# First node stage of a two-layer graph network: plain transposes, the split at PSUM, ReLU on ScalarE, the residual sum on GpSimd, the root for two tiles at once

## The chip, the cores and the metric

The kernel runs on one core of a Trainium2 chip. The metric is the device time of one execution in microseconds (us). The core has TensorE (PE in the profile; its weight loads are PEld), VectorE (DVE), ScalarE (ACT), GpSimd (POOL) and SyncE (SP), each with an instruction queue of its own that runs in order; they meet only at semaphores. In this kernel TensorE writes to PSUM, eight banks of 128 x 512 fp32, and everything else lies in SBUF or in the chip's DRAM.

## What is computed

10000 nodes with 512 features each, 10000 edges, two layers, each followed by a residual sum and a normalisation without learned scale:

```python
x = _layernorm(x + _L0_gnn_ref(x, edge_weight, W, b, edge_index))     # graph convolution
x = _layernorm(x + _L1_gnn_ref(x, src, dst, ...))                     # equivariant message layer

def _L0_gnn_ref(x, edge_weight, W, b, edge_index):
    ...
    norm = deg_inv_sqrt[src_all] * w_all * deg_inv_sqrt[dst_all]
    xp = x @ W
    out = segment_sum(xp[src_all] * norm[:, None], dst_all, N) + b    # self loops with weight 1
    return relu(out)

def _layernorm(x, eps=1e-05):
    return (x - mean(x)) / sqrt(var(x) + eps)
```

Only the part behind the segment sum of the first layer matters here. Since the sum and `@ W` commute, the kernel first sums the scaled neighbour rows into `sum0`, and then, node tile by node tile: z = sum0 + dis * x, y = relu(dis * (z @ W) + b) + x, x1 = layernorm(y).

## The kernel before

Nodes and edges are padded to 10240 = 80 tiles of 128 rows. There are five stages: constants and degrees, `edges0` (gather, TensorE combine, scatter-add into `sum0`), `nodes0` (the stage of the change), `edges1` (the second layer's messages, scatter-add into `sum1`) and `nodes1` (its node part). Each engine has its own program for each stage. `skewed` writes such a program as a software pipeline: in step s an engine does each of its parts for the tile s minus a lag, in the order in which the parts stand in its `nodes0` function. That order by hand is what sets when a part can run: an engine that waits holds up all that stands behind it.

`nodes0`, one tile a step. A lag is the number of steps behind the tile's load. All tiles are 128 x 512 fp32 unless said otherwise.

- SP: lag 0, loads `sl` (of `sum0`, ring of 4) and `xl` (of x, ring of 8), L366 and L368. Lag 8: stores x1 out of `res` to `x1_d` and to `sum1`, L372 and L373.
- DVE: lag 4, `pre`: L780, res = PSUM * dis + b. Lag 0, z: L786, sl = xl * dis + sl. Then again lag 4: L789, res = max(res, 0) + xl; L791 `bn_stats`; L793 `bn_aggr` into `mv`.
- ACT: lag 0, L567, z_hi = z rounded to fp32r. Lag 2: L556 and L561 copy the transposed high and low part from PSUM. Lag 5: L551 Ln and L559 Exp, the first guess of 1/sqrt(var + eps), 128 x 1. Lag 6: L571, the normalisation, res = res * scale + bias.
- POOL: lag 6, the five small operations of one Newton step on 128 x 1 (L458, L461, L463, L465, L467), then lag 0, z_lo = z - z_hi, L471.
- PE: lag 2, eight 128 x 128 fp32r multiplications with an identity (L984), four for z_hi and four for z_lo, into banks 0 to 3. Lag 3: twelve 128-row multiplications with 512 columns (L994): hi x Whi, hi x Wlo, lo x Whi for four chunks, into banks 4 to 7.

`Stage(sem, t, total)` counts the marks of a tile on one semaphore, `settle` waits for the engine's own last mark, `held` is a wait with a counting instruction behind it.

Of the kernel before, what the change touches and what calls it, by code (L numbers as in the profile page):

```python
# [85 lines left out]
def build(nc, x, src_cols, dst_cols, src_row, dst_row, weight, rbf, vec,  # L86
# [5 lines left out]
    with ExitStack() as ctx:  # L92
        def sb(name, shape, dt=F32):
            return ctx.enter_context(nc.sbuf_tensor(name, shape, dt))

        def sem(name):
            return ctx.enter_context(nc.semaphore(name))

        def ring(name, n, shape, dt=F32):
            return [sb(f"{name}{i}", shape, dt) for i in range(n)]  # L100
# [13 lines left out]
        ident_r = sb("ident_r", [P, P], F32R)  # L114
# [67 lines left out]
        sl, res, W0_s = ([b[:, q * D:(q + 1) * D] for b in node_mem] for q in range(3))  # L182
        xl = G
        z_hi, z_lo = (ring(name, 4, [P, D], F32R) for name in ("z_hi", "z_lo"))
        zT_hi, zT_lo = (ring(name, 2, [P, D], F32R) for name in ("zT_hi", "zT_lo"))
        stat = ring("stat", 4, [P, 6])
        mv = ring("mv", 4, [P, 2])
        tiny = ring("tiny", 4, [P, 8])
# [13 lines left out]
        msg_hi, msg_lo = z_hi, z_lo  # L202
# [63 lines left out]
        n_st = [sem(f"n_st{i}") for i in range(4)]  # L266
# [51 lines left out]
        K_RES, K_ROOT = 4, 5  # L318
# [7 lines left out]
        def _(sp_):  # L326
# [34 lines left out]
            def nodes0(s, u):  # L361
                a = u % 4
                if live(s, 0):
                    held(sp_, n_hi, s - 3)
                    held(sp_, n_lo, s - 3)
                    sp_.dma_start(sl[a], rows(sum0, s)).then_inc(n_sl[a], 16)  # L366
                    held(sp_, n_res, K_RES * (s - 7))
                    sp_.dma_start(xl[u], rows(x, s)).then_inc(n_xl[u], 16)  # L368
                if live(s, 8):
                    t = s - 8  # L370
# [4 lines left out]
            skewed(sp_, nodes0, 8, 8, unroll=8)  # L375
# [40 lines left out]
        def _(pool):  # L416
# [35 lines left out]
            def nodes0(s, u):  # L452
                if live(s, 6):

                    t, w, mean, var = s - 6, tiny[(u - 6) % 4], mv[(u - 6) % 4][:, 0:1], mv[(u - 6) % 4][:, 1:2]
# [7 lines left out]
                    st.mark(pool.tensor_scalar(w[:, 4:5], w[:, 3:4], -0.5, 1.5, ALU.mult, ALU.add))  # L463
                    st.settle(pool)
                    st.mark(pool.tensor_tensor(w[:, 5:6], w[:, 4:5], w[:, 2:3], ALU.mult))  # L465
                    held(pool, n_rstd, st.reached())
                    st.mark(pool.tensor_scalar(w[:, 6:7], mean, w[:, 5:6], -1.0, ALU.mult, ALU.mult))  # L467
# [39 lines left out]
        def _(act):  # L507
# [39 lines left out]
            def nodes0(s, u):  # L547
                if live(s, 5):
                    t, a = s - 5, (u - 5) % 4
                    act.wait_ge(n_res, K_RES * (t + 1))  # L550
                    act.activation(tiny[a][:, 1:2], mv[a][:, 1:2], ACT.Ln, bias=eps_c[:, :]).then_inc(n_rs, 1)  # L551
                if live(s, 2):
                    b = u % 2
                    act.wait_ge(n_tr, s - 1)
                    wait(act, n_mm, s - 3)
                    act.copy(zT_hi[b][:, :], bank[b][:, :]).then_inc(n_zT, 1)  # L556
                if live(s, 5):
                    act.wait_ge(n_rs, 2 * t + 1)
                    act.activation(tiny[a][:, 2:3], tiny[a][:, 1:2], ACT.Exp, scale=-0.5).then_inc(n_rs, 1)  # L559
                if live(s, 2):  # L560
                    act.copy(zT_lo[b][:, :], bank[2 + b][:, :]).then_inc(n_zT, 1)  # L561
                if live(s, 0):
                    a = u % 4
                    act.wait_ge(n_z, s + 1)
                    wait(act, n_tr, s - 3)
                    wait(act, n_lo, s - 3)
                    act.copy(z_hi[a][:, :], sl[a]).then_inc(n_hi, 1)  # L567
                if live(s, 6):
                    t, a = s - 6, (u - 6) % 4
                    act.wait_ge(n_rstd, K_ROOT * (t + 1))  # L570
                    act.activation(res[a], res[a], ACT.Identity, bias=tiny[a][:, 6:7], scale=tiny[a][:, 5:6]) \  # L571
                       .then_inc(n_x1, 1)

            skewed(act, nodes0, 6, 8, unroll=8)
# [87 lines left out]
        def _(dve):  # L662
# [20 lines left out]
            dve.tensor_scalar(ident_r[:, :], ident_i[:, :], 0.0, None, ALU.is_equal)  # L683
# [236 lines left out]
        def _(pe):  # L920
# [53 lines left out]
            def nodes0(s, u):  # L974

                if live(s, 2):
                    t, a, b = s - 2, (u - 2) % 4, u % 2
                    pe.wait_ge(n_hi, t + 1)
                    wait(pe, n_zT, 2 * (t - 1))
                    for part_, to in ((z_hi, bank[b]), (z_lo, bank[2 + b])):  # L980
                        if part_ is z_lo:
                            pe.wait_ge(n_lo, t + 1)
                        for c in range(4):
                            ins = pe.matmul(to[:, c * P:(c + 1) * P], part_[a][:, c * P:(c + 1) * P], ident_r[:, :],  # L984
                                            start=True, stop=True)
# [16 lines left out]
            pe.wait_ge(n_zT, 2 * T)  # L1002
            pe.wait_ge(n_res, K_RES * T)
# [117 lines left out]
```

## Time and profile before

| | |
|---|---|
| time, median of 3 runs | 1312.16 us (1312.09 to 1312.88) |
| the profiled execution, its own time | 1313.1 us |
| its span in the trace | 1311.3 us |
| first and last start of the `pre` operation (L780), 80 tiles | 360.5 and 655.7 us |
| PE, DVE, ACT, POOL busy in the whole span | 80%, 71%, 56%, 58% |
| TensorE clock, mean share of full speed | 0.896 |

The profile gives for each engine what ran when, and for each idle stretch what ended it. The shares of the whole span mix five stages with different limits. The stage of the change runs from about 349 to 662 us; it has to be read alone, and inside it one period of its loop. The start of an operation minus the start of the one before it on the same engine is what that one costs the engine; its duration is a little longer, since the end of one and the start of the next overlap.

### The profile page before, as it was taken

What the parts mean: (1) busy time and instruction counts of PE and PEld (TensorE: products, weight loads), DVE (VectorE), ACT (ScalarE), POOL (GpSimd) and SP (SyncE); (2) the same over time, 40 slices, a digit from 0 to 9 for tenths busy, and PEclk for the clock granted to TensorE, in tenths of its full rate; (3) what the DMA queues carried; (4) which work ended last, traced back from release to release, by engine and by line L of the source; (5) the groups of instructions that cost most, each with busy time, mean ns of one, the idle gap of its engine ahead of it and who ended that gap; (6) DMA issues with size and microseconds to landing.
All of it is one profiled execution on the core that took longest, in us unless ns stands there. A gap on an engine that the chain in (4) does not pass through costs nothing.

```text
span 1311.3 us, 27255 instructions
## 1 busy us (share of the span) xinstructions
PE 1049.4 (80%) x5208; PEld 783.2 (60%) x5208; DVE 928.9 (71%) x2936; ACT 735.9 (56%) x1852; POOL 756.5 (58%) x892
## 2 busy tenths in 40 slices
PE   7388778787599999999949999999999999514443
PEld 7343334343388888888738777776776777313332
DVE  8564354431188888888738888888888888529887
ACT  0111111111266667666648777777777777428887
POOL 0257777778367777777725666766766776410000
PEclk9998889898699999999969999999999999855555
DMA  9979999999757777777633556555555555369998
GB/s 366 412 193 218 222 217 212 211 222 181 205 187 258 265 258 263 262 260 264 207 114 80 104 107 103 107 103 104 104 104 107 102 105 107 51 148 328 347 354 288
DMA packets 164962, 257.37 MB, mean 196 GB/s; under 512 B 17514, under 2 KB 81470, under 8 KB 164926
## 3 DMA queue, kind: packets, MB, share of 16 engines
q0 software_dynamic: 35840, 83.91, 34.3%
q1 hardware_dynamic: 111902, 144.78, 33.9%
q10 hardware_dynamic: 17184, 28.32, 5.7%
q8 instruction: 10, 0.16, 0.1%
q14 instruction: 26, 0.21, 0.1%
HBM read 129.00 MB, written 127.93 MB: 196 GB/s over the span
## 4 chain that ended last, share of the span: by engine, by line
DMA 34%; issue 19%; POOL 10%; PE 3%; POOLq 2%; ACT 2%; DVE 2%; SPq 2%; ACTq 0%; DVEq 0%
DMA sum<-R_mem,sidx 30%; POOL tiny L458 3%; DMA node_mem<-sum 3%; POOL tiny L461 2%; POOL tiny L465 1%; PE bank L994 1%; POOL tiny L463 1%; DMA sum<-R_mem,sidx_all 1%; POOL z_lo L471 1%; POOLq L313 1%; POOL sum L444 1%; POOLq L314 1%; SPq L408 1%; ACT node_mem L649 1%; POOL tiny L467 0%
## 5 line engine op out<-in xcount | busy, mean ns | idle before, releaser
L963 PE MATMUL bank<-G_mem,edge_mem 128*128 128x512 f32 x400 | 196.4, 650 | 49.1 <-DMA G_mem<-x,src_i 49.1
L500 POOL DMA_INDIRECT sum<-R_mem,sidx x80 | 127.1, 1589 | 138.7 <-DMA sum<-R_mem,sidx 95.6
L534 ACT COPY R_mem<-bank 128x512 f32<-128x512 f32 x80 | 46.9, 586 | 227.5 <-PE bank L963 201.8
L963 PEld LDWEIGHTS bank<-G_mem,edge_mem 128*128 128x128 f32 x400 | 81.8, 209 | 151.2 <-issue 134.5
L485 POOL TENSOR_TENSOR z_lo<-edge_mem,z_hi 128x512 fp32r<-128x512 f32 x80 | 145.3, 1816 | 18.8 <-ACT z_hi L608 18.8
L444 POOL DMA_INDIRECT sum<-R_mem,sidx_all x80 | 127.5, 1594 | 45.1 <-issue 26.1
L994 PE MATMUL bank<-W0h,zT_hi 128*128 128x512 f32 x320 | 133.3, 417 | 0.8 <-ACT zT_lo L561 0.8
L994 PE MATMUL bank<-W0l,zT_hi 128*128 128x512 f32 x320 | 126.0, 394 | 0.0
L994 PE MATMUL bank<-W0h,zT_lo 128*128 128x512 f32 x320 | 126.0, 394 | 0.0
L761 DVE TENSOR_SCALAR edge_mem<-trow,dst_f,coef 128x512 f32<-128x512 int32 (+1 forms) x80 | 31.8, 459 | 130.2 <-PE bank L963 120.5
L571 ACT ACTIVATE node_mem<-node_mem,tiny 128x512 f32<-128x512 f32 x80 | 65.4, 817 | 92.1 <-POOL tiny L467 92.1
L471 POOL TENSOR_TENSOR z_lo<-node_mem,z_hi 128x512 fp32r<-128x512 f32 x80 | 103.7, 1297 | 21.1 <-ACT z_hi L567 21.1
L618 ACT ACTIVATE G_mem<-G_mem,ew 128x512 f32<-128x512 f32 x80 | 57.8, 723 | 95.2 <-DMA G_mem<-x_d,gidx 95.1
L786 DVE SCALAR_TENSOR_TENSOR node_mem<-G_mem,dis,node_mem 128x512 f32<-128x512 f32 x80 | 82.0, 1025 | 40.8 <-DMA G_mem<-x 40.8
L811 DVE TENSOR_SCALAR proj<-G_mem,Y 128x128 f32<-128x128 f32 x80 | 85.6, 1070 | 29.6 <-ACT G_mem L618 27.6
L1067 PE MATMUL bank<-ident,node_mem 128*128 128x128 f32 x80 | 27.4, 446 | 91.3 <-DVE node_mem L892 91.3
L492 POOL DMA_INDIRECT G_mem<-x_d,gidx x80 | 85.8, 1072 | 23.6 <-issue 17.0
L1031 PE MATMUL bank<-h,Wf_s 128*128 128x128 f32 x640 | 92.1, 288 | 3.2 <-DVE edge_mem L853 2.9
L430 POOL DMA_INDIRECT G_mem<-x,src_i x80 | 79.5, 994 | 24.2 <-issue 21.2
L1025 PE MATMUL bank<-edge_mem,Winv 128*128 128x512 f32 x160 | 90.8, 650 | 0.0
L780 DVE SCALAR_TENSOR_TENSOR node_mem<-bank,dis,b_s 128x512 f32<-128x512 f32 x80 | 60.0, 750 | 38.3 <-DMA sum<-node_mem 29.6
L1031 PEld LDWEIGHTS bank<-h,Wf_s 128*128 128x128 f32 x640 | 82.3, 198 | 5.7 <-issue 4.8
(161 smaller groups left out, 2896.2 us busy)
## 6 DMA issues: line engine op xcount, KB each, us to landing
sum<-zeros ACTq DMA_DIRECT2D x42, 512.0 KB, 11.4
node_mem<-sum SPq DMA_DIRECT2D x80, 256.0 KB, 2.7
G_mem<-x SPq DMA_DIRECT2D x80, 256.0 KB, 2.8
x_d<-node_mem SPq DMA_DIRECT2D x80, 256.0 KB, 2.1
sum<-node_mem SPq DMA_DIRECT2D x80, 192.0 KB, 2.0
out<-G_mem SPq DMA_DIRECT2D x20, 512.0 KB, 4.3
out<-R_mem SPq DMA_DIRECT2D x20, 512.0 KB, 4.4
G_mem<-sum SPq DMA_DIRECT2D x20, 384.0 KB, 5.1
```

The lines of the kernel that those rows point to most:

```text
L430: pool.indirect_dma_start(G[k][:, :], None, x, bass.IndirectOffsetOnAxis(ap=src_i[:, t:t + 1], axis=0)) \
L444: pool.indirect_dma_start(sum0, bass.IndirectOffsetOnAxis(ap=sidx[:, t:t + 1], axis=0), R[t % 8][:, :], None, compute_op=ALU.add).then_inc ...
L471: pool.tensor_tensor(z_lo[u][:, :], sl[u], z_hi[u][:, :].bitcast(F32), ALU.subtract).then_inc(n_lo, 1)
L485: pool.tensor_tensor(msg_lo[a][:, :], msg[a % 2][:, P:640], msg_hi[a][:, :].bitcast(F32), ALU.subtract) \
L492: pool.indirect_dma_start(G3[a][:, :], None, x1_d, bass.IndirectOffsetOnAxis(ap=gidx3[a][:, :], axis=0)) \
L500: pool.indirect_dma_start(sum1, bass.IndirectOffsetOnAxis(ap=sidx3[a][:, :], axis=0), R3[a][:, :], None, compute_op=ALU.add).then_inc(f_sc ...
L786: dve.scalar_tensor_tensor(sl[c], xl[u], dis[:, bass.ds(s, 1)], sl[c], ALU.mult, ALU.add).then_inc(n_z, 1)
L811: sj.mark(dve.tensor_scalar(proj[a][:, :], gv[:, :, 0], Y[:, bass.ds(t, 1), 0], None, ALU.mult))
L963: ins = pe.matmul(bank[j][:, :], M[c][q][:, j * P:(j + 1) * P], G[4 * c + q][:, :], start=(q == 3), stop=(q == j))
L994: ins = pe.matmul(bank[4 + a][:, :], zt[b][:, c * P:(c + 1) * P], w[:, c, :], start=(c == 0 and k == 0), stop=(c == 3 and k == 2))
L1025: pe.matmul(bank[2][:, :], Winv[:, :], rawT[b][:, 0:512], start=True, stop=True)
L1031: ins = pe.matmul(bank[4][:, q * P:(q + 1) * P], Wf2_s[:, base:base + 255:2], h[b][:, :], start=True, stop=True)
```

## The change

In `nodes0` of the first layer only:

- z is no longer split before the transposes. PE transposes z itself as fp32, four `transpose` instructions with `ident` instead of eight multiplications with `ident_r`; lag 1. The bank ring for it is 0 to 3, one bank for a tile.
- ACT copies the bank to zT_hi (rounding); DVE computes zT_lo = bank - zT_hi. z_hi, z_lo, ACT's L567 and L561 and POOL's L471 are gone; zT_hi and zT_lo are rings of 4.
- DVE writes `pre` (L780's operation); ACT does ReLU on `res` in place; POOL adds xl in place; DVE then takes `bn_stats` and `bn_aggr`. DVE's L789 is gone.
- Ln, Exp and the Newton step run once for a pair of tiles, on 128 x 2; seven small operations on POOL with six waits in between or before, no pointer scalars.
- `res` has 8 buffers, the stores have 8 semaphores, stores come at lag 9, the normalisation at lag 8.

The order within a step is new on each engine:

```diff
@@ gpsimd, nodes0
-                if live(s, 6):
-                    st = Stage(n_rstd, t, K_ROOT)
-                    held(pool, n_res, K_RES * (t + 1))
-                    st.mark(pool.tensor_scalar(w[:, 0:1], var, EPS, None, ALU.add))
-                    held(pool, n_rstd, st.reached())
-                    held(pool, n_rs, 2 * (t + 1))
-                    st.mark(pool.tensor_scalar(w[:, 3:4], w[:, 2:3], w[:, 2:3], w[:, 0:1], ALU.mult, ALU.mult))
...
-                if live(s, 0):
-                    pool.wait_ge(n_hi, s + 1)
-                    wait(pool, n_tr, s - 3)
-                    pool.tensor_tensor(z_lo[u][:, :], sl[u], z_hi[u][:, :].bitcast(F32), ALU.subtract).then_inc(n_lo, 1)
+                if live(s, 6) and u % 2:
+                    t, a = s - 7, (u - 7) // 2 % 4
+                    held(pool, n_mv, t + 2)
+                    st.mark(pool.tensor_scalar(w[:, 0, :], var, EPS, None, ALU.add))
+                    st.mark(pool.tensor_scalar(w[:, 7, :], mean, -1.0, None, ALU.mult))
+                    held(pool, n_rs, 2 * (g + 1))
+                    st.mark(pool.tensor_tensor(w[:, 3, :], w[:, 2, :], w[:, 2, :], ALU.mult))
+                    st.settle(pool)
+                    st.mark(pool.tensor_tensor(w[:, 4, :], w[:, 3, :], w[:, 0, :], ALU.mult))
+                    held(pool, n_rstd, st.reached())
+                    st.mark(pool.tensor_scalar(w[:, 3, :], w[:, 4, :], -0.5, 1.5, ALU.mult, ALU.add))
+                    st.settle(pool)
+                    st.mark(pool.tensor_tensor(w[:, 5, :], w[:, 3, :], w[:, 2, :], ALU.mult))
+                    st.settle(pool)
+                    st.mark(pool.tensor_tensor(w[:, 6, :], w[:, 7, :], w[:, 5, :], ALU.mult))
+                if live(s, 4):
+                    pool.wait_ge(n_rel, t + 1)
+                    pool.tensor_tensor(res[a], res[a], xl[a], ALU.add).then_inc(n_sum, 1)
@@ scalar, nodes0 (Ln and Exp of the pair stand ahead of and behind the zT_hi copy)
+                    act.wait_ge(n_tr, t2 + 1)
+                    wait(act, n_mm, t2 - 3)
+                    act.copy(zT_hi[b][:, :], bank[b][:, :]).then_inc(n_hi, 1)
...
+                if live(s, 4):
+                    act.wait_ge(n_pre, t4 + 1)
+                    act.activation(res[c], res[c], ACT.Relu).then_inc(n_rel, 1)
+                if live(s, 8):
+                    act.wait_ge(n_rstd, K_ROOT * (g8 + 1))
+                    act.activation(res[c], res[c], ACT.Identity, ...).then_inc(n_x1, 1)
@@ vector, nodes0
                 if live(s, 0):
                     dve.scalar_tensor_tensor(sl[c], xl[u], dis[:, bass.ds(s, 1)], sl[c], ALU.mult, ALU.add).then_inc(n_z, 1)
+                if live(s, 5):
+                    dve.wait_ge(n_sum, t + 1)
+                    dve.bn_stats(stat[c][:, :], res[a]).then_inc(n_bn, 1)
+                if live(s, 2):
+                    dve.wait_ge(n_hi, t + 1)
+                    wait(dve, n_mm, t - 3)
+                    dve.tensor_tensor(zT_lo[b][:, :], bank[b][:, :], zT_hi[b][:, :].bitcast(F32), ALU.subtract).then_inc(n_lo, 1)
+                if live(s, 5):
+                    if k == 0:
+                        held(dve, n_x1, t - 6)
+                    held(dve, n_bn, t + 1)
+                    dve.bn_aggr(mv[b][:, k, :], stat[a % 4][:, :]).then_inc(n_mv, 1)
                 if live(s, 4):
-                    st.settle(dve)
-                    st.mark(dve.scalar_tensor_tensor(res[a], res[a], 0.0, xl[(u - 4) % 8], ALU.max, ALU.add))
...
+                    dve.wait_ge(n_mm, t + 1)
+                    wait(dve, n_st[a], 32 * turn(t, a, 8))
+                    dve.scalar_tensor_tensor(res[a], bank[4 + c][:, :], dis[:, bass.ds(t, 1)], b0_s[:, :],
+                                             ALU.mult, ALU.add).then_inc(n_pre, 1)
@@ tensor, nodes0 (lag 1: four transposes; lag 3: the eight products with zT_hi, a wait for n_lo, the four with zT_lo)
+                    for c in range(4):
+                        ins = pe.transpose(bank[a][:, c * P:(c + 1) * P], sl[a][:, c * P:(c + 1) * P], ident[:, :])
```

## Rows read from the trace of the kernel before

**Rows 1.** Windows: us, busy us (instructions) by engine, TensorE clock, DMA share, GB/s.
```profile
500.00:620.00 120.00, 120.00 (x641) 102.89 (x640) 102.19 (x161) 81.94 (x193) 89.80 (x193) 1.00 0.77 262
```

**Rows 2.** Chain of work that ended last, 499 to 508 us, shares by line.
```profile
by line: issue 58.2%; POOL tiny L458 11.9%; POOL tiny L461 8.7%; POOL z_lo L471 4.9%; POOL tiny L465 4.5%; POOL tiny L463 4.3%; POOLq L313 3.4%; POOL tiny L467 2.1%; POOLq L314 2.1%; POOLq L74 0.7%; POOLq L469 0.7%
```

**Rows 3.** Timeline of POOL: start, duration (us), engine, line, operation; idle before.
```profile
500.61 0.53 POOL L458 TENSOR_SCALAR tiny<-mv 128x1 f32<-128x1 f32 x1
...
502.08 0.19 POOL L463 TENSOR_SCALAR tiny<-tiny 128x1 f32<-128x1 f32 x1 [0.20 <-POOL tiny L461]
...
502.76 0.26 POOL L467 TENSOR_SCALAR tiny<-mv,tiny 128x1 f32<-128x1 f32 x1 [0.21 <-POOL tiny L465]
502.98 1.31 POOL L471 TENSOR_TENSOR z_lo<-node_mem,z_hi 128x512 fp32r<-128x512 f32 x1
504.37 0.53 POOL L458 TENSOR_SCALAR tiny<-mv 128x1 f32<-128x1 f32 x1
```

**Rows 4.** Timeline of PE, same stage: first transpose, first product, next tile's transpose.
```profile
504.35 0.56 PE L984 MATMUL bank<-ident_r,z_hi 128*128 128x128 f32 x4
...
505.23 0.49 PE L994 MATMUL bank<-W0h,zT_hi 128*128 128x512 f32 x1
...
508.07 0.56 PE L984 MATMUL bank<-ident_r,z_hi 128*128 128x128 f32 x4
```

**Rows 5.** Timeline of PE in `edges1`: two plain fp32 transposes, back to back.
```profile
904.82 0.27 PE L1017 MATMUL bank<-ident,proj 128*128 128x128 f32 x1
...
904.93 0.27 PE L1018 MATMUL bank<-ident,G_mem 128*128 128x128 f32 x1
```

**Rows 6.** Timeline of DVE in `nodes0`, 388 to 392 us.
```profile
388.32 0.68 DVE L789 SCALAR_TENSOR_TENSOR node_mem<-node_mem,G_mem 128x512 f32<-128x512 f32 x1
389.04 0.69 DVE L791 BATCH_NORM_STATS2 stat<-node_mem 128x6 f32<-128x512 f32 x1
389.88 0.18 DVE L793 BATCH_NORM_AGGREGATE mv<-stat 128x2 f32<-128x6 f32 x1 [0.15 <-DVE stat L791]
390.01 0.75 DVE L780 SCALAR_TENSOR_TENSOR node_mem<-bank,dis,b_s 128x512 f32<-128x512 f32 x1
390.68 1.40 DVE L786 SCALAR_TENSOR_TENSOR node_mem<-G_mem,dis,node_mem 128x512 f32<-128x512 f32 x1
```

**Rows 7.** Lines by form (count, busy us, mean ns, idle): two DVE operations with a PSUM operand.
```profile
L900 DVE TENSOR_TENSOR R_mem<-bank,node_mem 128x256 f32<-128x256 f32 x20 | 8.4, 419 | 0.2
L853 DVE SCALAR_TENSOR_TENSOR edge_mem<-bank,bf_c,edge_mem 128x384 f32<-128x384 f32 x70 | 42.6, 608 | 0.0
```

**Rows 8.** Timeline of the stage's start: the first tile from DVE to ACT to POOL.
```profile
348.85 0.75 DVE L786 SCALAR_TENSOR_TENSOR node_mem<-G_mem,dis,node_mem 128x512 f32<-128x512 f32 x1 [38.92 <-DMA G_mem<-x]
349.64 0.62 ACT L567 CAST z_hi<-node_mem 128x512 fp32r<-128x512 f32 x1 [7.87 <-DVE node_mem L786]
...
350.34 1.26 POOL L471 TENSOR_TENSOR z_lo<-node_mem,z_hi 128x512 fp32r<-128x512 f32 x1 [11.11 <-ACT z_hi L567]
```

**Rows 9.** Instructions of line 571: count, duration min/median/max (ns), first and last start.
```profile
L571 ACT ACTIVATE node_mem<-node_mem,tiny x80: 813/817/820, 371.1 to 661.1; 128x512 f32<-128x512 f32 x80
```

**Rows 10.** Timeline of POOL: the subtraction that runs beside L786 of rows 6.
```profile
390.23 1.31 POOL L471 TENSOR_TENSOR z_lo<-node_mem,z_hi 128x512 fp32r<-128x512 f32 x1
```

**Rows 11.** Instructions of line 780: count, duration min/median/max (ns), first and last start.
```profile
L780 DVE SCALAR_TENSOR_TENSOR node_mem<-bank,dis,b_s x80: 749/750/753, 360.5 to 655.7; 128x512 f32<-128x512 f32 x80
```

**Rows 12.** Timeline of PE at the stage's start, low clock: two products in a row.
```profile
356.94 0.63 PE L994 MATMUL bank<-W0l,zT_hi 128*128 128x512 f32 x1
...
357.36 0.63 PE L994 MATMUL bank<-W0h,zT_lo 128*128 128x512 f32 x1
```

**Rows 13.** Windows of `edges0` and `edges1`, columns as in rows 1.
```profile
190.00:200.00 10.00, 6.19 (x8) 2.64 (x9) 2.98 (x16) 1.17 (x2) 7.88 (x7) 0.51 1.03 220
720.00:740.00 20.00, 18.28 (x113) 13.97 (x113) 16.69 (x60) 15.24 (x41) 12.74 (x11) 1.00 0.57 108
```

More of the change, by code:

```diff
@@ L181, in build @@
         node_mem = ring("node_mem", 4, [P, 4 * D])
-        sl, res, W0_s = ([b[:, q * D:(q + 1) * D] for b in node_mem] for q in range(3))
+        sl, W0_s = ([b[:, q * D:(q + 1) * D] for b in node_mem] for q in (0, 2))
+        res = [b[:, q * D:(q + 1) * D] for q in (1, 2) for b in node_mem]
         xl = G
-        z_hi, z_lo = (ring(name, 4, [P, D], F32R) for name in ("z_hi", "z_lo"))
-        zT_hi, zT_lo = (ring(name, 2, [P, D], F32R) for name in ("zT_hi", "zT_lo"))
+        zT_hi, zT_lo = (ring(name, 4, [P, D], F32R) for name in ("zT_hi", "zT_lo"))
         stat = ring("stat", 4, [P, 6])
-        mv = ring("mv", 4, [P, 2])
-        tiny = ring("tiny", 4, [P, 8])
+        mv = ring("mv", 4, [P, 2, 2])
+        tiny = ring("tiny", 4, [P, 8, 2])
         trow3 = ring("trow3", 4, [P, P], I32)
@@ L201, in build @@
         M3 = ring("M3", 4, [P, P], F32R)
-        msg_hi, msg_lo = z_hi, z_lo
+        msg_hi, msg_lo = zT_hi, zT_lo
         junk3 = ring("junk3", 4, [P, P])
@@ L265, in build @@
         n_x1 = sem("n_x1")
-        n_st = [sem(f"n_st{i}") for i in range(4)]
+        n_st = [sem(f"n_st{i}") for i in range(8)]
         f_trow = [sem(f"f_trow{i}") for i in range(4)]
@@ L373, in nodes0 @@
                     sp_.dma_start(sum1[bass.ds(t * P, P), C:D], res[a][:, C:D]).then_inc(n_st[a], 16)
[L375 removed]
+            skewed(sp_, nodes0, 9, 16, unroll=8)
             def edges1(s, u):
@@ L478, in _ @@
+                    st.settle(pool)
+                    st.mark(pool.tensor_tensor(w[:, 6, :], w[:, 7, :], w[:, 5, :], ALU.mult))
+                if live(s, 4):
+                    t, a = s - 4, (u - 4) % 8
+                    pool.wait_ge(n_rel, t + 1)
+                    pool.tensor_tensor(res[a], res[a], xl[a], ALU.add).then_inc(n_sum, 1)
+            skewed(pool, nodes0, 8, 16, unroll=8)
+            for u in range(8):
+                held(pool, n_st[u], 32 * (T // 8))
             held(pool, s_zero1, 16 * (T4 + 4))
@@ L547, in nodes0 @@
             def nodes0(s, u):
[L548 to L551, printed above, removed]
-                if live(s, 2):
[L553 to L571, printed above, removed]
+                tail = live(s, 6) and u % 2
+                if tail:
+                    t, a = s - 7, (u - 7) // 2 % 4
+                    g = t // 2 if isinstance(t, int) else (t - (u - 7) % 8) // 2 + a
+                    act.wait_ge(n_mv, t + 2)
+                    act.activation(tiny[a][:, 1, :], mv[a][:, :, 1], ACT.Ln, bias=eps_c[:, :]).then_inc(n_rs, 1)
@@ new lines, in nodes0 @@
+                if live(s, 2):
+                    t2, b = s - 2, (u - 2) % 4
+                    act.wait_ge(n_tr, t2 + 1)
+                    wait(act, n_mm, t2 - 3)
+                    act.copy(zT_hi[b][:, :], bank[b][:, :]).then_inc(n_hi, 1)
+                if tail:
+                    act.wait_ge(n_rs, 2 * g + 1)
+                    act.activation(tiny[a][:, 2, :], tiny[a][:, 1, :], ACT.Exp, scale=-0.5).then_inc(n_rs, 1)
+                if live(s, 4):
+                    t4, c = s - 4, (u - 4) % 8
+                    act.wait_ge(n_pre, t4 + 1)
+                    act.activation(res[c], res[c], ACT.Relu).then_inc(n_rel, 1)
@@ L572, in nodes0 @@
+                if live(s, 8):
+                    t8, c = s - 8, u % 8
+                    k, b = c % 2, c // 2
+                    g8 = t8 // 2 if isinstance(t8, int) else (t8 - c) // 2 + b
+                    act.wait_ge(n_rstd, K_ROOT * (g8 + 1))
+                    act.activation(res[c], res[c], ACT.Identity, bias=tiny[b][:, 6, k:k + 1], scale=tiny[b][:, 5, k:k + 1]) \
                        .then_inc(n_x1, 1)
-            skewed(act, nodes0, 6, 8, unroll=8)
+            skewed(act, nodes0, 8, 16, unroll=8)
@@ L974, in nodes0 @@
             def nodes0(s, u):
[L976 to L985, printed above, removed]
+                if live(s, 1):
+                    t, a = s - 1, (u - 1) % 4
+                    pe.wait_ge(n_z, t + 1)
+                    wait(pe, n_lo, t - 3)
+                    for c in range(4):
+                        ins = pe.transpose(bank[a][:, c * P:(c + 1) * P], sl[a][:, c * P:(c + 1) * P], ident[:, :])
@@ L986, in nodes0 @@
                     ins.then_inc(n_tr, 1)
                 if live(s, 3):
-                    t, a, b = s - 3, (u - 3) % 4, (u - 3) % 2
-                    pe.wait_ge(n_zT, 2 * (t + 1))
-                    wait(pe, n_res, K_RES * (t - 3))
+                    t, a = s - 3, (u - 3) % 4
+                    pe.wait_ge(n_hi, t + 1)
+                    wait(pe, n_pre, t - 3)
                     for c in range(4):
-                        for k, (zt, w) in enumerate(((zT_hi, W0h), (zT_hi, W0l), (zT_lo, W0h))):
-                            ins = pe.matmul(bank[4 + a][:, :], zt[b][:, c * P:(c + 1) * P], w[:, c, :],
-                                            start=(c == 0 and k == 0), stop=(c == 3 and k == 2))
+                        for w in (W0h, W0l):
+                            pe.matmul(bank[4 + a][:, :], zT_hi[a][:, c * P:(c + 1) * P], w[:, c, :],
+                                      start=(c == 0 and w is W0h), stop=False)
@@ L996, in nodes0 @@
+                    pe.wait_ge(n_lo, t + 1)
+                    for c in range(4):
+                        ins = pe.matmul(bank[4 + a][:, :], zT_lo[a][:, c * P:(c + 1) * P], W0h[:, c, :],
+                                        start=False, stop=(c == 3))
                     ins.then_inc(n_mm, 1)
             skewed(pe, nodes0, 3, 8)
-            pe.wait_ge(n_zT, 2 * T)
-            pe.wait_ge(n_res, K_RES * T)
+            pe.wait_ge(n_lo, T)
+            pe.wait_ge(n_pre, T)
             pe.wait_ge(s_wTc, 3)
```

51 lines of the change are left out of this document (20 added, 31 removed).

## The prediction, made from the kernel before

> **What bounds the kernel now.** I read the windows by stage first, since only one stage changes. Inside `nodes0` TensorE is busy all the time at its full clock, DVE 85% of it, POOL 75%, DMA 77% [rows 1]. A full TensorE looks like the bound, but its ends are modelled, so I looked at the chain of work next. It runs through POOL alone: its five small operations and z_lo; the large share called issue is the time in which POOL works off z_lo, and it always ends where L458 starts [rows 2]. The timeline of POOL gives the period: L458 starts at 500.61 and again at 504.37, 3.76 us. Of this 2.37 us go to the small operations (to 502.98) and 1.39 to z_lo [rows 3]. PE needs 0.88 us for eight multiplications with the identity and 2.84 us for twelve products, 3.72 together, so it stands only just behind POOL [rows 4]. Over the stage: `pre` starts first at 360.5 and last at 655.7, (655.7 - 360.5)/79 = 3.737 us a tile [rows 11]. That is the period I have to replace.
>
> **The parts, and what each engine would need.** All by start-to-start distances, which are a duration less some 0.08 us (`pre` lasts 0.75 and the next starts 0.67 later [rows 6]).
>
> PE: four plain transposes start 0.11 us apart in the later stage [rows 5], so about 0.44 plus 0.1 of run-in in place of 0.88; with 2.84 for the products, 3.4 us. The products' order doesn't matter for their sum.
>
> POOL: z_lo goes (-1.39), the addition comes. It is the same form, two SBUF operands, 128 x 512, and z_lo took 1.26 alone and 1.31 beside DVE [rows 8, 10]: 1.30, or 1.39 start to start. The small operations: five became seven, but for two tiles. A first one of 0.53 at most, a second of 0.26 (like L467), a wait of 0.20, then five at (502.76 - 502.08)/2 = 0.34 each [rows 3] with their waits: 2.7 us a pair. Twice the width (128 x 2) I cost at nothing: one element a row takes 0.19 us (L463), 512 take 1.31, so an element more is about 2 ns [rows 3]. POOL then needs 1.39 + 1.35 = 2.7 us a tile instead of 3.76.
>
> ACT: loses the z_hi cast (0.62) and the zT_lo copy, gains ReLU, SBUF to SBUF, 128 x 512. The nearest rows are the z_hi cast, 0.62 [rows 8], and the normalisation with two pointer operands, 0.82 [rows 9]. ReLU has no such operands: 0.62, bounds 0.57 to 0.82. ACT was busy 82 of 120 us, 2.6 of 3.75 a tile, so it has room [rows 1].
>
> DVE: loses L789 (0.68), gains zT_lo with one PSUM operand. 256 columns of this operation take 0.419 us; 384 columns of a three-operand one take 0.608 and 512 take 0.75, so 1.1 ns a column [rows 6, 7]. 0.419 + 256 x 1.07 ns = 0.69 us, 0.60 start to start; bounds 0.53 and 0.67 (from 0.75). DVE's sum is z 0.66, bn_stats 0.61, zT_lo 0.60, bn_aggr 0.12, pre 0.67 = 2.7 us, up to 3.3 where z waits for POOL.
>
> DMA moves the same bytes: 0.77 of 3.75 us, so 2.9 us a tile at least. Its waits (loads ahead by some steps, the store's 8 buffers for 4) get looser; the wait of `pre` for the store goes, and it bound nothing, as the chain is POOL's.
>
> So by work alone the tile would take 3.4 us (PE).
>
> **What the new order makes of it.** The parts of one tile t now pass from engine to engine and back. DVE writes pre(t) as the last thing of step t+4. ACT's ReLU(t) waits for it, POOL's addition(t) waits for ReLU(t), and DVE's bn_stats(t) waits for the addition. But bn_stats(t) stands in step t+5, with only z between it and pre(t). DVE runs in order, so zT_lo(t+3), bn_aggr(t) and pre(t+1) queue behind that wait. This closes a loop, one tile a turn, that no engine's speed but only the sum of latencies sets. Before, ReLU and residual followed pre on DVE itself (L789) and the statistics too, so no such loop was there. From pre's start:
>
> pre 0.75 + hand-over to ACT 0.04 (349.60 to 349.64) + ReLU 0.62 + hand-over to POOL 0.08 (350.26 to 350.34) [rows 8] + addition 1.30 + hand-over to DVE 0.05 (between those two) + bn_stats 0.61 (0.69 less 0.08) + zT_lo 0.60 + bn_aggr 0.13 (389.88 to 390.01 [rows 6]) = 4.18 us.
>
> z (0.66 from pre's start, lasting 0.75 alone) is over 1.41 us after pre's start, before the addition begins at 1.49: hidden. The other members are ready in time: ACT's zT_hi copy comes after ReLU and the normalisation, some 1.4 us behind ReLU's end, while DVE needs it 1.4 + 0.6 behind it. PE has 3.4 us of work in 4.2.
>
> Where the paired root falls: in odd steps POOL does it between two additions. The loop leaves it 4.18 - 1.30 = 2.88 us, and it needs 0.09 + 2.7. It just fits, with 0.1 us to spare. What could push it out is DVE's z: L786 lasted 1.40 instead of 0.75 us while z_lo ran beside it, and ended 0.54 behind z_lo's end [rows 6, 8, 10]; so one of the two was held off by the other. In the new order z starts about 2.05 us behind the end of an addition, where the last small operations run; one of them held off for up to 0.7 us would end the root near 3.1 and delay every second addition by 0.2 to 0.3. I take half of that, 0.07 a tile on the mean of both parities. The Trainium skill (SBUF — State Buffer, section "SBUF: two separate sides") says that DVE with two SBUF inputs and GpSimd share a port pair as an exclusive lock, the loser blocking for a whole instruction. The 1.40 us agree with that. By this rule the larger figure would hold: a small operation caught behind z costs all the rest of z.
>
> Period: 4.18 + 0.07 = 4.25 us.
>
> Head and tail: pre(0) starts about when it did (360.5; one fewer dependence on POOL, perhaps a us earlier). After pre(79) now come 0.79 + 0.70 + 1.35 + 0.70 + 0.15 + 0.18 + the root's 2.2 + two normalisations 1.6 = 7.7 us; before, from 655.7 to the end of the last L571 at 661.9, 6.2 [rows 9, 11]. A us either way: 0.
>
> **Sum.** 79 x (4.25 - 3.737) = +40.5 us against the profiled execution's 1313.1, whose own span is 1311.3 and which lies 0.9 above the median of the runs. On the median: 1312.2 + 40.5 = **1352.7 us**, 3.1% slower. Other stages: nothing changes in them but the names of two buffer rings and four more waits, under a us.
>
> **Rivals.**
>
> 1. No loop binds. If the wait of bn_stats were met early (a queue deeper than I think, or if I misread which tile the addition serves), PE sets 3.4 us: 79 x (3.4 - 3.737) = -27, 1286 us. For it: every engine's sum falls. Against: the indices, t+4 for pre and addition, t+5 for bn_stats, with z alone between. Chance 0.05, and 0.02 that loop and savings happen to balance within 0.2%.
>
> 2. The root sticks out on odd steps. If z catches it, or ReLU is as slow as the normalisation (0.82), or zT_lo takes 0.67, the turn is 4.18 + 0.20 + 0.07 + 0.06 (addition 1.36) + up to 0.25 = 4.76 us: +81, 1393 us. It decides as soon as the root takes over 2.8 us. Chance 0.13, together with the milder forms of it from 1370 upwards.
>
> 3. TensorE's clock falls. It will idle about 0.85 us of each 4.25, where it didn't idle before. At the low level (1.2 GHz) products start 0.42 us apart instead of 0.23 [rows 12], 12 x 0.42 + 1 = 6.1 us a tile, over the loop. For it: in `edges0` the clock was 0.51 in a stretch in which PE was busy 62% and its loads 26% [rows 13]. Against: in `edges1` loads were busy 70% and the clock held at 1.00 [rows 13], and the new stage has 16 loads of some 0.19 us in 4.25, 71%. With half of the stage at the low level: 79 x 0.5 x (6.1 - 4.25) = +73 more, about 1425 us. Chance 0.05. The Trainium skill (TensorE: Matmul & The Clock Gate, section "Part 4: PE-mode transpose") says that transposes of this mode don't count as activity for the clock; before they were ordinary multiplications. No row here isolates that; `edges1` has five such transposes a tile and held its clock.
>
> The forecast itself has 0.75. Its own range: all hand-overs at nothing and ReLU and zT_lo at their lower ends give 4.0 us, +21, 1333; ReLU at 0.75 with a late root gives 4.47, +58, 1370. Rivals 1 and 3 are left out of the range, most of rival 2 is taken in: **1332 to 1390**. A measurement of this kernel can tell 0.2%, 2.6 us, from no change. Faster by more than that 0.05, within it 0.02, slower 0.93.
>
> **What would show it.** In the profile after: the starts of `pre` 4.2 to 4.3 us apart; DVE idle before bn_stats, released by POOL's addition, some 1.4 us in each step (2.84 less 1.41); the chain going DVE, ACT, POOL, DVE; POOL idle before the addition in even steps and hardly in odd ones; PE with idle of 0.8 us a tile at a clock of 1.00. Wrong if DVE's bn_stats doesn't wait (rival 1), if POOL has no idle and odd steps are much longer than even ones (rival 2), or if the clock in the stage is below 0.9 (rival 3).

## The result

The changed kernel takes 1374.72 us, median of four runs (1372.81 to 1376.3), the kernel before beside it 1312.52 us: a ratio of 1.0473 (95% interval 1.0452 to 1.0494), 4.7% slower. Forecast were 1352.7 us and a range of 1332 to 1390. The sign and the range held; of the +62 us the forecast had 40.5, and the loop that it named turned out to be the second limit, not the first.

All of it lies in the stage of the change. The first and the last `pre` answer to [rows 11]; the operation has moved to line 803 (columns: count, duration min/median/max in ns, first and last start in us):

```profile
L803 DVE SCALAR_TENSOR_TENSOR node_mem<-bank,dis,b_s x80: 710/718/752, 358.5 to 717.3; 128x512 f32<-128x512 f32 x80
```

(717.3 - 358.5)/79 = 4.54 us a tile instead of 3.737; 79 x 0.805 = 63.6 us, and the span grew by 63.2 (1311.3 to 1374.5). The window that answers to [rows 1]:

```profile
500.00:520.00 20.00, 15.33 (x72) 11.24 (x70) 10.79 (x20) 9.62 (x19) 9.75 (x19) 1.00 0.62 216
```

No engine is at its limit: PE is busy 77%, DVE 54%, ACT 48%, POOL 49%, DMA 62%, and the clock is still full. So something waits in a circle. Who waited for whom in the stage (380 to 660 us; total us, times, longest), the last line from the same view of SyncE's DMA queue:

```profile
ACT node_mem L570 <- DVE node_mem L803: 161.4, 61, 3.2
POOL node_mem L476 <- ACT node_mem L570: 130.2, 61, 3.7
DVE node_mem L782 <- DMA G_mem<-x: 113.1, 61, 2.6
...
SPq L316 <- ACT node_mem L576: 136.1, 61, 3.0
```

The forecast had DVE waiting before bn_stats. It waits before z (L782) instead, for a load, once in each of 61 steps. In [rows 6] z followed pre without a gap. And SyncE's queue waits for ACT's normalisation (L576). The timelines of the four queues over two turns:

```profile
499.26 0.72 DVE L803 SCALAR_TENSOR_TENSOR node_mem<-bank,dis,b_s 128x512 f32<-128x512 f32 x1
...
500.01 0.63 ACT L570 ACTIVATE node_mem<-node_mem 128x512 f32<-128x512 f32 x1 [2.52 <-DVE node_mem L803]
500.55 0.80 ACT L576 ACTIVATE node_mem<-node_mem,tiny 128x512 f32<-128x512 f32 x1
...
501.59 0.35 SPq L373 DMA_DIRECT2D x_d<-node_mem  x1
502.14 0.36 SPq L374 DMA_DIRECT2D sum<-node_mem  x1
502.76 0.35 SPq L367 DMA_DIRECT2D node_mem<-sum  x1
503.30 0.35 SPq L369 DMA_DIRECT2D G_mem<-x  x1
...
505.29 1.30 POOL L476 TENSOR_TENSOR node_mem<-node_mem,G_mem 128x512 f32<-128x512 f32 x1 [3.27 <-ACT node_mem L570]
...
506.45 0.75 DVE L782 SCALAR_TENSOR_TENSOR node_mem<-G_mem,dis,node_mem 128x512 f32<-128x512 f32 x1 [1.90 <-DMA G_mem<-x]
507.12 0.69 DVE L786 BATCH_NORM_STATS2 stat<-node_mem 128x6 f32<-128x512 f32 x1
507.72 0.68 DVE L791 TENSOR_TENSOR zT_lo<-bank,zT_hi 128x512 fp32r<-128x512 f32 x1
508.31 0.17 DVE L798 BATCH_NORM_AGGREGATE mv<-stat 128x2 f32<-128x6 f32 x1
508.40 0.72 DVE L803 SCALAR_TENSOR_TENSOR node_mem<-bank,dis,b_s 128x512 f32<-128x512 f32 x1
```

By the starts: pre to ReLU 0.75, ReLU 0.54, normalisation to the first store 1.04, two stores and the load of `sl` to the load of `xl` 1.71, load to z 3.15, z 0.67, bn_stats 0.60, zT_lo 0.59, bn_aggr 0.09, and the second pre: 499.26 to 508.40, 9.14 us. Between them lies one more pre (503.83), so the circle has two turns: 4.57 us a tile. The order of the queues closes it: SyncE issues the load of step s behind the store that waits for the normalisation of ACT's step s-2, and that normalisation stands behind ReLU, which waits for pre of the same step. The addition ends at 506.59, 0.53 us before bn_stats starts, so z's wait for the load is the one that ends last here; what either is worth, the runs below show. (The chain-of-work view does not help: between 500 and 514 us it stays on POOL, 73.6% "issue" and 19.7% addition.)

### The profile page after: what moved, and what is told of

Read it like the earlier page. It is cut to its first block, busy times and chain, and to the rows that moved or that the text cites. A ratio compares the mean times of both kernels' runs of the same rounds, so it can differ in the third digit from the quotient of the medians.

```text
span 1374.5 us, 25149 instructions
## 1 busy us (share of the span) xinstructions
PE 1026.2 (75%) x4888; PEld 735.1 (53%) x4888; DVE 894.5 (65%) x2935; ACT 685.7 (50%) x1692; POOL 701.7 (51%) x772
## 4 chain that ended last, share of the span: by engine, by line
DMA 33%; issue 25%; POOL 7%; PE 4%; DVE 3%; ACT 2%; SPq 1%; POOLq 1%; DVEq 0%; ACTq 0%
DMA sum<-R_mem,sidx 28%; POOL node_mem L476 4%; DMA node_mem<-sum 3%; DMA G_mem<-x 1%; PE bank L974 1%; DVE stat L919 1%; DMA sum<-R_mem,sidx_all 1%; PE bank L1036 1%; POOL tiny L462 1%; PE bank L1042 1%; POOL tiny L466 1%; POOL tiny L470 0%; POOL tiny L472 0%; POOL tiny L468 0%; SPq L409 0%
## 5 line engine op out<-in xcount | busy, mean ns | idle before, releaser
L476 POOL TENSOR_TENSOR node_mem<-node_mem,G_mem 128x512 f32<-128x512 f32 x80 | 103.3, 1291 | 188.2 <-ACT node_mem L570 188.2
L782 DVE SCALAR_TENSOR_TENSOR node_mem<-G_mem,dis,node_mem 128x512 f32<-128x512 f32 x80 | 65.4, 818 | 170.6 <-DMA G_mem<-x 170.6
L570 ACT ACTIVATE node_mem<-node_mem 128x512 f32<-128x512 f32 x80 | 50.6, 632 | 212.9 <-DVE node_mem L803 212.9
L490 POOL TENSOR_TENSOR zT_lo<-edge_mem,zT_hi 128x512 fp32r<-128x512 f32 x80 | 145.3, 1816 | 19.1 <-ACT zT_hi L613 19.1
L992 PE MATMUL bank<-ident,node_mem 128*128 128x128 f32 x320 | 53.3, 290 | 100.1 <-DVE node_mem L782 100.1
L992 PEld LDWEIGHTS bank<-ident,node_mem 128*128 128x128 f32 x320 | 35.0, 143 | 131.9 <-issue 73.3
L1078 PE MATMUL bank<-ident,node_mem 128*128 128x128 f32 x80 | 27.4, 446 | 90.9 <-DVE node_mem L903 90.9
L1027 PE MATMUL bank<-ident,G_mem 128*128 128x128 f32 x240 | 48.3, 311 | 51.0 <-DVE proj L838 25.4
```

Source lines behind the costliest of these rows:

```text
L476: pool.tensor_tensor(res[a], res[a], xl[a], ALU.add).then_inc(n_sum, 1)
L490: pool.tensor_tensor(msg_lo[a][:, :], msg[a % 2][:, P:640], msg_hi[a][:, :].bitcast(F32), ALU.subtract) \
L992: ins = pe.transpose(bank[a][:, c * P:(c + 1) * P], sl[a][:, c * P:(c + 1) * P], ident[:, :])
```

## The experiments

Theory L: the loads' circle of two turns binds. Rival S, the prediction's own: the circle of the statistics (pre, ReLU, addition, bn_stats, zT_lo, bn_aggr, pre) binds. Periods are (last less first start of pre)/79 throughout. Ratios are to the kernel before beside each run, 1309.6 to 1311.7 us.

**Stores one step later.**

```diff
@@ sync, nodes0
-                if live(s, 9):
-                    t, a = s - 9, (u - 9) % 8
+                if live(s, 10):
+                    t, a = s - 10, (u - 10) % 8
-            skewed(sp_, nodes0, 9, 16, unroll=8)
+            skewed(sp_, nodes0, 10, 16, unroll=8)
```

> The changed kernel with the stores of x1 one step later in SyncE's order (lag 10 for 9), nothing else. Theory L (the loads bind: load(s) is queued behind the store that waits for the normalisation of step s-2, so two turns must hold 9.14 us: pre, ReLU, normalisation, stores, load, landing, z, bn_stats, zT_lo, bn_aggr, pre): the load then follows the normalisation of step s-3, the loop has three turns (3.05 us), and the loop of the statistics takes over: pre 0.75, ReLU 0.71 up to the addition's start, 1.30, hand-over 0.05, bn_stats 0.60, zT_lo 0.59, bn_aggr 0.09 = 4.09, with hand-overs 4.1 to 4.25 us a tile; about 1374 - 79 x 0.37 = 1345 us (1338 to 1351). DVE would then wait before bn_stats for POOL, not before z for a DMA. Rival S (the statistics' loop alone binds at 4.54, z only starts late because it has time): no change, 1370 to 1378. Rival P (GpSimd and VectorE block each other on the sums with two SBUF operands): no change either.

Measured: 1338.19 us, ratio to before 1.0196 (1.0161 to 1.0231). Period 4.06 us (358.8 to 679.8). This edit in SyncE's order alone gives back 36 of the 62 us. Its waits (400 to 640 us) and its timeline:

```profile
DVE stat L786 <- POOL node_mem L476: 82.4, 59, 1.4
```

```profile
501.20 0.72 DVE L803 SCALAR_TENSOR_TENSOR node_mem<-bank,dis,b_s 128x512 f32<-128x512 f32 x1
501.83 0.75 DVE L782 SCALAR_TENSOR_TENSOR node_mem<-G_mem,dis,node_mem 128x512 f32<-128x512 f32 x1
...
501.95 0.63 ACT L570 ACTIVATE node_mem<-node_mem 128x512 f32<-128x512 f32 x1 [1.96 <-DVE node_mem L803]
...
502.66 1.28 POOL L476 TENSOR_TENSOR node_mem<-node_mem,G_mem 128x512 f32<-128x512 f32 x1 [0.83 <-ACT node_mem L570]
...
503.98 0.69 DVE L786 BATCH_NORM_STATS2 stat<-node_mem 128x6 f32<-128x512 f32 x1 [1.40 <-POOL node_mem L476]
504.59 0.67 DVE L791 TENSOR_TENSOR zT_lo<-bank,zT_hi 128x512 fp32r<-128x512 f32 x1
505.18 0.17 DVE L798 BATCH_NORM_AGGREGATE mv<-stat 128x2 f32<-128x6 f32 x1
505.27 0.72 DVE L803 SCALAR_TENSOR_TENSOR node_mem<-bank,dis,b_s 128x512 f32<-128x512 f32 x1
```

z follows pre at once, and DVE's wait has moved to bn_stats, for the addition: 1.40 us a step. This is the picture that the prediction drew for the changed kernel, and its terms: 0.75 + 0.71 + 1.28 + 0.04 + 0.61 + 0.59 + 0.09 = 4.07 against the 4.18 of the forecast. Rival S as the only limit is out, and so is rival P, which wanted no change.

**Statistics last, behind pre** (bn_stats and bn_aggr keep their lag of 5, the addition gets a step more).

```diff
@@ vector, nodes0: order in a step
-                z(s); bn_stats(s-5); zT_lo(s-2); bn_aggr(s-5); pre(s-4)
+                z(s); zT_lo(s-2); pre(s-4); bn_stats(s-5); bn_aggr(s-5)
```

> The changed kernel with bn_stats and bn_aggr of a tile moved behind pre in VectorE's step, nothing else: the addition gets a whole step more. Theory L: bn_stats and bn_aggr leave the two-turn loop of the loads, which keeps 9.14 - 0.60 - 0.09 = 8.45, 4.23 us a tile: 1374 - 79 x 0.31 = 1350 us (1343 to 1356), with VectorE waiting before z for the DMA. Theory S (statistics' loop alone binds): it is gone, TensorE's 3.4 to 3.5 us remain, about 1290 us.

Measured: 1342.78 us, ratio 1.0257 (1.0207 to 1.0306); 4.12 us a tile (356.0 to 681.4). DVE waits before z for the load again (400 to 640 us):

```profile
DVE node_mem L782 <- DMA G_mem<-x: 72.5, 56, 1.9
```

With the circle of the statistics gone the loads' circle stays and is shorter by what left it. It was 0.11 us a tile shorter than worked out, and the time lies at the lower edge of the expected range (1343). In its timeline two loads reach z 2.80 and 2.90 us after their issue instead of 3.15, while first store to load takes 2.22 and 1.84 instead of 1.71; how these add up over the stage I did not settle.

**The addition for one column only.**

```diff
-                    pool.tensor_tensor(res[a], res[a], xl[a], ALU.add).then_inc(n_sum, 1)
+                    pool.tensor_tensor(res[a][:, 0:1], res[a][:, 0:1], xl[a][:, 0:1], ALU.add).then_inc(n_sum, 1)
```

> The changed kernel with the residual sum on GpSimd done for one column of 512 only; the other 511 columns lack the residual, so this output isn't the reference's. The addition's 1.30 us shrink to about 0.2, all waits stay. Theory L: the addition is not in the loop that binds, 4.54 us a tile stay, 1370 to 1376 us. Theory S, and the prediction's own reading: the loop through the addition gets 1.1 us shorter, 3.4 us a tile, 1285 to 1295 us.

Measured, one run: 1364.73 us, 5 below the expected range; 4.42 us a tile (360.3 to 709.1) where S wants 3.4. Taking 1.1 us out of the addition (0.19 us are left) gives back 0.13: it is not in the circle that binds. The starts of z alternate, 4.10 and 4.87 us apart, which shows the two turns:

```profile
498.13 0.75 DVE L782 SCALAR_TENSOR_TENSOR node_mem<-G_mem,dis,node_mem 128x512 f32<-128x512 f32 x1 [2.36 <-DMA G_mem<-x]
...
502.23 0.75 DVE L782 SCALAR_TENSOR_TENSOR node_mem<-G_mem,dis,node_mem 128x512 f32<-128x512 f32 x1 [1.43 <-DMA G_mem<-x]
...
507.10 0.75 DVE L782 SCALAR_TENSOR_TENSOR node_mem<-G_mem,dis,node_mem 128x512 f32<-128x512 f32 x1 [2.20 <-DMA G_mem<-x]
```

The circle from 498.13 to 507.10 is 8.97 us long instead of 9.14, and nearly all of the difference is the load: issued at 504.11, it came through to z 2.99 us later instead of 3.15. The stage's mean, 8.83 us for two turns, is shorter still; that rest stays open.

**Both edits together.**

> Stores one step later and the statistics behind pre, together. Theory L plus the statistics' loop as the second limit: neither binds any more, TensorE does with 3.4 us a tile (2.84 + 0.55), up to 3.55 where VectorE and GpSimd hold each other off: 1374 - 79 x 1.1 = 1287 us (1284 to 1298), faster than the kernel before by 1.5 to 2%. If either edit alone already gives all of it, or both together less than their sum, theory L has a wrong part.

Measured: 1316.86 us, ratio 1.0043 (1.0026 to 1.0059); 3.78 us a tile (359.7 to 658.4), not 3.4: this expectation missed by 30 us. The edits give back 37 and 32 us alone and 58 together, less than their sum, which the expectation had named as a sign that theory L lacks something. It lacked a third limit. Neither circle is left, and TensorE idles (busy 89% from 500 to 600 us). The timeline:

```profile
503.05 1.29 POOL L476 TENSOR_TENSOR node_mem<-node_mem,G_mem 128x512 f32<-128x512 f32 x1 [0.25 <-ACT node_mem L570]
...
503.27 1.62 DVE L782 SCALAR_TENSOR_TENSOR node_mem<-G_mem,dis,node_mem 128x512 f32<-128x512 f32 x1
504.81 0.68 DVE L787 TENSOR_TENSOR zT_lo<-bank,zT_hi 128x512 fp32r<-128x512 f32 x1
...
507.12 1.63 DVE L782 SCALAR_TENSOR_TENSOR node_mem<-G_mem,dis,node_mem 128x512 f32<-128x512 f32 x1
```

DVE, busy 93% from 500 to 600 us, has no gap but the short one before bn_aggr; z lasts 1.62 us instead of 0.75 (1.619 is also the median over the 80 tiles). It starts 0.22 us behind the addition and ends 0.55 behind its end. ReLU starts when pre ends, the addition 0.7 later, and bn_stats and bn_aggr take just that time, so z meets the addition in every step. By sharing, both would get longer; here the addition keeps its 1.29 and z carries all of it. The Trainium skill (SBUF — State Buffer, "SBUF: two separate sides") has this rule for VectorE with two SBUF inputs against GpSimd, an exclusive lock that is held for an instruction; the trace agrees (1.62 us). Two runs test it.

**Both edits, the addition for one column only.**

> The two edits together (stores one step later, statistics behind pre), with the residual sum done for one column of 512 only; the other 511 columns lack the residual, so this output isn't the reference's. Theory B: nothing on GpSimd holds z off but the small operations, z lasts 0.75 to 0.85 instead of 1.62, VectorE needs 3.0 us, TensorE binds: 3.4 to 3.5 us a tile, 1285 to 1294 us. Rival D: 3.78 us stay, 1313 to 1320 us.

Measured, one run: 1279.84 us, 5 below the expected range, 3.30 us a tile (359.2 to 619.8); z is back at 0.75:

```profile
L782 DVE SCALAR_TENSOR_TENSOR node_mem<-G_mem,dis,node_mem x80: 741/752/753, 350.2 to 608.2; 128x512 f32<-128x512 f32 x80
```

**Stores one step later, statistics at lag 6 right behind z**, so that z runs while ReLU does and is over when the full addition starts.

```diff
@@ vector, nodes0: order in a step (stores at lag 10)
-                z(s); bn_stats(s-5); zT_lo(s-2); bn_aggr(s-5); pre(s-4)
+                z(s); bn_stats(s-6); bn_aggr(s-6); zT_lo(s-2); pre(s-4)
```

> Stores one step later, and the statistics at lag 6 right behind z, so that VectorE's order is z, bn_stats, bn_aggr, zT_lo, pre. No loop through the addition is left, and z (two SBUF operands) starts right behind pre, while ReLU still runs, so it should be over when GpSimd's addition starts. Theory B (in both edits together 3.78 us a tile were left because z ran beside the addition and lasted 1.62 us instead of 0.75): z back at 0.75 to 0.9, VectorE needs 0.67 + 0.75 + 0.10 + 0.60 + 0.65 = 2.8 us, TensorE binds with 3.4, GpSimd's root may slip by some tenths: 3.4 to 3.6 us a tile, 1316 - 79 x 0.3 = 1293 us (1286 to 1301). Rival D (DMA or TensorE bound at 3.78, z only stretched because there was time): no change from the two edits, 1313 to 1320 us.

Measured: 1292.54 us, ratio 0.9863 (0.9839 to 0.9888), 3.48 us a tile (361.0 to 636.1). With the whole addition in place the median of z is back at 0.744 us:

```profile
L782 DVE SCALAR_TENSOR_TENSOR node_mem<-G_mem,dis,node_mem x80: 741/744/1720, 352.2 to 622.6; 128x512 f32<-128x512 f32 x80
```

It is the same work as in the changed kernel, 6% faster than it and 1.4% faster than before. Rival D, that DMA or TensorE set 3.78, falls. What is left are long odd steps. Timelines of POOL, ACT and DVE:

```profile
500.56 1.31 POOL L476 TENSOR_TENSOR node_mem<-node_mem,G_mem 128x512 f32<-128x512 f32 x1
503.78 1.29 POOL L476 TENSOR_TENSOR node_mem<-node_mem,G_mem 128x512 f32<-128x512 f32 x1 [1.92 <-ACT node_mem L570]
...
506.93 0.60 POOL L472 TENSOR_TENSOR tiny<-tiny 128x2 f32<-128x2 f32 x1
507.56 1.30 POOL L476 TENSOR_TENSOR node_mem<-node_mem,G_mem 128x512 f32<-128x512 f32 x1
```

```profile
504.66 0.30 ACT L558 ACTIVATE tiny<-mv,eps_c 128x2 f32<-128x2 f32 x1 [0.25 <-DVE mv L791]
504.86 0.57 ACT L563 CAST zT_hi<-bank 128x512 fp32r<-128x512 f32 x1
...
505.46 0.69 DVE L796 TENSOR_TENSOR zT_lo<-bank,zT_hi 128x512 fp32r<-128x512 f32 x1 [0.83 <-ACT zT_hi L563]
```

Additions start 3.22 and 3.78 us apart. In the long step ACT waits for bn_aggr before Ln (L558), the zT_hi copy is queued behind Ln, and DVE's zT_lo waits for that; POOL too has no gap there.

**Ln behind the zT_hi copy**, added to the last version.

```diff
@@ scalar, nodes0: order in an odd step
-                Ln(pair); copy zT_hi; Exp(pair); ReLU; normalisation
+                copy zT_hi; Ln(pair); Exp(pair); ReLU; normalisation
```

> The version with the stores one step later and the statistics at lag 6, and in ScalarE's odd steps Ln moved behind the zT_hi copy, nothing else. Theory: in the odd steps ScalarE waited 0.25 us for bn_aggr before Ln, with the zT_hi copy behind it, and VectorE's zT_lo waited 0.83 us for that copy; odd steps lasted 3.78 us, even ones 3.22. With the copy first, odd steps come down towards TensorE's 3.23: 3.25 to 3.35 us a tile, 1292.5 - 79 x 0.18 = 1278 us (1274 to 1284). Rival (odd steps are set by GpSimd, whose addition and root follow each other without a gap for 3.78 us): no change, 1289 to 1296 us, unless the even steps get shorter in return.

Measured: 1274.26 us, ratio 0.9728 (0.9697 to 0.9758), 3.26 us a tile (363.0 to 620.3), 2.7% faster than before. TensorE is busy again all the time, and DMA is the next:

```profile
500.00:600.00 100.00, 99.84 (x495) 81.84 (x493) 87.74 (x155) 62.68 (x123) 68.20 (x140) 1.00 0.89 302
```

The rival is half right: POOL's long step stays (additions start at 497.89, 501.59 and 504.34, 3.70 and 2.75 us apart), and the short ones give way. This trace also has the block the other way round, z first and the addition behind it at 1.85 us:

```profile
507.57 1.85 POOL L476 TENSOR_TENSOR node_mem<-node_mem,G_mem 128x512 f32<-128x512 f32 x1
...
507.51 0.75 DVE L781 SCALAR_TENSOR_TENSOR node_mem<-G_mem,dis,node_mem 128x512 f32<-128x512 f32 x1 [0.68 <-DMA G_mem<-x]
```

**The kernel before with its stores one step earlier**: the same loss of lead, without the change.

```diff
@@ sync, nodes0 of the kernel before
-                if live(s, 8):
-                    t = s - 8
+                if live(s, 7):
+                    t, a = s - 7, (u - 7) % 4
-            skewed(sp_, nodes0, 8, 8, unroll=8)
+            skewed(sp_, nodes0, 7, 8, unroll=8)
```

> The kernel before with its stores of x1 one step earlier in SyncE's order (lag 7 for 8), nothing else: the same loss of one step of lead for the loads that the change brought. In the kernel before it makes a loop of two turns: z 0.75, z_hi 0.62, normalisation 0.82, stores and load issue 2.1, landing 3.15 = 7.4 us, 3.7 a tile, and one of three turns through the root on GpSimd, 11.3 us, 3.77. Theory L: 3.75 to 3.9 us a tile, 1312 to 1325 us; the wait of VectorE before z for the DMA, absent before, appears. Without such a loop: no such wait, 1311 to 1314 us.

Measured: 1343.95 us, ratio 1.0261 (1.0232 to 1.029); 4.18 us a tile (359.3 to 689.5). The mechanism shows, the wait that the kernel before did not have (400 to 620 us):

```profile
DVE node_mem L786 <- DMA G_mem<-x: 51.4, 52, 1.6
```

The size missed: 3.75 to 3.9 was expected. In this trace a small operation of the root (L461) has a median of 1.15 us; in the kernel before it has 0.38:

```profile
L461 POOL TENSOR_SCALAR tiny<-tiny x80: 340/1153/1422, 367.6 to 693.4; 128x1 f32<-128x1 f32 x80
499.52 1.12 POOL L461 TENSOR_SCALAR tiny<-tiny 128x1 f32<-128x1 f32 x1 [0.37 <-ACT tiny L559]
```

The one at 499.52 runs beside z and L789 on DVE and ends at 500.64, 0.14 us behind L789. The normalisation waits for the root behind it, the stores for the normalisation, the load for the stores: from z at 499.15 that way round to z at 508.02 are 8.87 us for two turns. I had added the terms without the block. That it makes up the whole 0.3 us is argued, not shown.

## Why the prediction was right, and where it was not

The range held partly by luck. Its upper end, from 1370 on, was there for a paired root that sticks out, and the time landed there for another reason. The sign held for the reason given: with the loads out of the way the circle that the prediction named makes the kernel 2% slower by itself.

- **The bound before** and the period of 3.737 us: nothing spoke against them, and no run tests them. TensorE's share after the change was forecast as 3.4 us and came out as 3.26 in the last version, since the four transposes cost 0.41 us up to the first product (498.20 to 498.61 in the changed kernel) and not 0.55.
- **The circle of the statistics** is real and was sized well. With the loads out of the way it sets 4.06 us a tile against 4.18 forecast (4.25 with the root). ReLU with its hand-over took 0.71 (0.70 forecast), the addition 1.28 to 1.30 (1.30), zT_lo 0.67 (0.69). The lower end of the range was added wrongly: 4.18 without its hand-overs (0.17) and with the lower ends of ReLU and zT_lo (0.05 and 0.07) is 3.89, not 4.0, so by its own terms the range began near 1324, not 1332.
- **The step that failed** is the sentence on DMA, that its waits "get looser". I looked at the ring sizes and at the store buffers, and not at the queue: the store's lag grew from 8 to 9, but the normalisation's from 6 to 8, so the loads behind that store lost one step of lead (from step s-3 to s-2 of ACT), and the normalisation now stands behind ReLU, which waits for DVE. Following that queue step by step would have shown it, from these rows of the kernel before (timelines of ACT and SyncE's queue; the last line is the page's, KB each and median us to landing):

```profile
503.06 0.82 ACT L571 ACTIVATE node_mem<-node_mem,tiny 128x512 f32<-128x512 f32 x1 [1.19 <-POOL tiny L467]
504.11 0.36 SPq L372 DMA_DIRECT2D x_d<-node_mem  x1
505.97 0.35 SPq L368 DMA_DIRECT2D G_mem<-x  x1
G_mem<-x SPq DMA_DIRECT2D x80, 256.0 KB, 2.8
```

  With the prediction's other terms: pre and hand-over 0.79, ReLU 0.54, normalisation to store 1.05, store to load 1.86, landing 2.8, z 0.66, bn_stats 0.61, zT_lo 0.60, bn_aggr 0.13, together 9.04 us for two turns, 4.52 a tile; 9.14 and 4.54 were measured. That missing circle is the difference of 22 us between 1352.7 and 1374.7 (79 x (4.54 - 4.25) = 23).
- **The paired root** (rival 2) does not stick out. It took 2.28 us (506.67 to 508.95, below) instead of 2.7, and 0.9 us were left behind it. The 0.07 us for it were for nothing. Doubling the width cost nothing: six of the seven operations take 0.19 to 0.22 us, as with one column. The first, 0.61 us here, runs beside z; where nothing of the kind runs beside it (last version, 505.72) it takes 0.22, so the 0.53 us that the prediction took for it came with a block of the same kind.

```profile
506.67 0.61 POOL L461 TENSOR_SCALAR tiny<-mv 128x2 f32<-128x2 f32 x1
507.36 0.22 POOL L462 TENSOR_SCALAR tiny<-mv 128x2 f32<-128x2 f32 x1
...
508.75 0.20 POOL L472 TENSOR_TENSOR tiny<-tiny 128x2 f32<-128x2 f32 x1
509.87 1.30 POOL L476 TENSOR_TENSOR node_mem<-node_mem,G_mem 128x512 f32<-128x512 f32 x1 [0.92 <-ACT node_mem L570]
```

- **No circle** (rival 1) was wrong for this kernel, and its price was about right for one in which it holds: forecast 3.4 us and 1286, measured 3.26 and 1274 once three orders were changed.
- **The clock** (rival 3) stayed at 1.00 with TensorE busy 77% in the window above and 74% from 380 to 700 us. Four of its sixteen instructions a tile are transposes of the plain kind; the rule of the Trainium skill that these don't count (TensorE: Matmul & The Clock Gate, "Part 4: PE-mode transpose") made no difference that these runs show.
- **DVE and POOL blocking each other** was weighed only for the small operations. In the changed kernel it costs next to nothing, since z starts late (median 0.752 us); it became the limit as soon as the circles were gone.

## What to carry to other kernels

Moving work to idle engines could buy 0.5 us a tile here (3.26 for 3.74) and as first ordered cost 0.8 (4.54), because in a hand-ordered pipeline a value that went from one engine through two others and back had only z to hide behind, and because the loads behind a waiting store in SyncE's queue inherited its wait. After a change of lags, write down for every queue which step each wait belongs to, close each circle and divide its length by its turns, loads included. And place VectorE's operations with two SBUF operands where GpSimd does not run.

## What the runs showed of the hardware

- An instruction of GpSimd with SBUF operands and one of VectorE with two of them do not share: the later one's duration in the profile contains the rest of the earlier (z 1.62 for 0.75 us, addition 1.85 for 1.30), with no wait shown. An overlap of 0.14 us at the end of an addition (z at 506.45 in the changed kernel) cost nothing. `pre`, with one operand in PSUM, keeps its 0.75 us beside GpSimd's z_lo in the kernel before (503.13, beside z_lo at 502.98 [rows 3, 11]).
- The TensorE clock held at full speed through some 340 us (360 to 700) in which it idled about a quarter of the time, in pieces of about 1.1 us.
- A two-operand addition of 128 x 512 fp32 takes GpSimd 1.29 us; an operation on 128 x 2 takes it 0.19 to 0.22, with 0.07 to 0.2 more where it waits for the one before.
